# Three passes of rounded halves for the scores and values of a fused transformer's first attention

## The reference

```python
q = rms_norm((x @ wq).reshape(B, L, 16, 128), q_norm_w); k = rms_norm((x @ wk).reshape(B, L, 4, 128), k_norm_w)
v = (x @ wv).reshape(B, L, 4, 128)                        # x is the layer-normed x
k_ctx, v_ctx = rms_norm(h_ctx_kv @ wk_ctx), h_ctx_kv @ wv_ctx      # 64 context rows
q, k = rope(q), rope(k)
k_full, v_full = [k_ctx; k], [v_ctx; v]                   # 64 + 512 keys, each KV head for 4 query heads
scores = einsum('blhd,bmhd->bhlm', q, k_full) / sqrt(128) + causal mask over the 512
out = einsum('bhlm,bmhd->blhd', softmax(scores), v_full)
x = x + tanh(g_xattn[0]) * (out.reshape(B, L, 2048) @ wo)
```

## Time and profile before

| | us |
|---|---|
| median of three runs | 1883.88 |
| the profiled execution | 1885.15 |
| its span | 1883.4 |
| PE busy | 1771.8 (94%) |
| DVE busy | 1093.9 (58%) |
| ACT busy | 1041.9 (55%) |
| POOL busy | 961.5 (51%) |

### The profile page before, as it was taken

How to read it: one execution, slowest core, us unless ns; L and a number is a source line. 1 busy time by engine, 2 the same in 40 slices (tenths; PEclk the granted TensorE clock), 3 DMA queues, 4 the chain that set the end, 5 groups by cost and what they waited for, 6 DMA issues and landing times. The chain is left out here.

```text
span 1883.4 us, 27617 instructions
## 1 busy us (share of the span) xinstructions
PE 1771.8 (94%) x9732; PEld 1313.5 (70%) x9732; DVE 1093.9 (58%) x2271; ACT 1041.9 (55%) x2318; POOL 961.5 (51%) x864
## 2 busy tenths in 40 slices
PE   7899999999999999999998999989999778879998
PEld 4677777777777777777775888879899656644443
DVE  5554544456445664456655658633433668868886
ACT  3666666655555555555554322136656367857875
POOL 5644565444654445554441100038888356657774
PEclk9999999999999999999999999999999989999999
DMA  7111111211011111011121200157889660000000
GB/s 248 58 48 46 51 36 46 69 33 52 36 40 37 51 53 52 20 34 52 53 68 44 109 23 23 45 183 227 231 224 278 173 162 1 1 6 18 23 23 23
DMA packets 113607, 141.30 MB, mean 75 GB/s; under 512 B 38000, under 2 KB 68720, under 8 KB 113280
## 3 DMA queue, kind: packets, MB, share of 16 engines
q1 hardware_dynamic: 106304, 122.76, 20.7%
q0 software_dynamic: 7168, 16.78, 4.2%
HBM read 104.91 MB, written 29.36 MB: 71 GB/s over the span
## 5 line engine op out<-in xcount | busy, mean ns | idle before, releaser
L767 POOL TENSOR_TENSOR a_xcl<-xT,a_xch 128x512 fp32r<-128x512 f32 x64 | 82.9, 1295 | 282.5 <-ACT a_xch L565 282.5
L876 PE MATMUL a_S<-a_kT,a_qT 128*128 128x288 f32 (+3 forms) x640 | 207.8, 423 | 7.0 <-ACT a_qT L598 5.4
L683 DVE TENSOR_REDUCE a_nmax<-a_S 128x1 f32<-128x192 f32 (+3 forms) x256 | 138.2, 550 | 55.6 <-PE a_S L877 55.2
L934 PE MATMUL a_A<-a_pT,a_vf 128*128 128x512 f32 x320 | 167.0, 604 | 0.9 <-ACT a_pT L586 0.8
L571 ACT ACTIVATE a_pr_odd<-a_S,a_nmax 128x320 f32<-128x320 f32 (+1 forms) x128 | 80.8, 632 | 147.3 <-DVE a_nmax L683 146.0
L876 PEld LDWEIGHTS a_S<-a_kT,a_qT 128*128 128x128 f32 x640 | 115.6, 189 | 52.8 <-issue 23.6
L120 PE MATMUL a_A<-a_wlo,a_xch 128*128 128x512 f32 x256 | 147.3, 575 | 2.7 <-DVE a_qT L679 2.6
L571 ACT ACTIVATE a_pr_even<-a_S,a_nmax 128x192 f32<-128x192 f32 (+1 forms) x128 | 67.2, 527 | 121.2 <-DVE a_nmax L683 120.8
L1592 POOL TENSOR_TENSOR e_wlo<-expert_raw,e_whi 128x1408 fp32r<-128x1408 f32 x31 | 100.4, 3238 | 50.4 <-ACT e_whi L1764 48.3
L2508 PE MATMUL f_HH<-w12T,f_f_xqT 128*128 128x512 bf16 x512 | 120.0, 382 | 4.5 <-DVE a_reco L2322 2.4
L120 PE MATMUL a_A<-a_wlo,a_oth 128*128 128x512 f32 x256 | 112.1, 438 | 7.8 <-DVE a_otl L723 7.8
(11 more groups left out here) (409 smaller groups left out, 5227.6 us busy)
## 6 DMA issues: line engine op xcount, KB each, us to landing
a_pw<-in_L_ffn_w_dram SPq DMA_DIRECT2D x96, 256.0 KB, 2.9
expert_raw<-in_L_ffn_w_gate_dram SPq DMA_DIRECT2D x16, 704.0 KB, 7.6
expert_raw<-in_L_ffn_w_up_dram SPq DMA_DIRECT2D x16, 704.0 KB, 9.7
expert_raw<-in_L_ffn_w_down_dram SPq DMA_DIRECT2D x16, 512.0 KB, 10.3
tern<-a_tern SPq DMA_DIRECT2D x48, 128.0 KB, 1.9
x_res<-in_x_dram SPq DMA_DIRECT2D x4, 1024.0 KB, 9.3
a_raw<-in_L_xattn_wq_dram SPq DMA_DIRECT2D x4, 1024.0 KB, 6.6
a_raw<-in_L_xattn_wo_dram SPq DMA_DIRECT2D x4, 1024.0 KB, 5.4
```

The costliest lines, as they stand in the source:

```text
L683: ve.tensor_reduce(nmax[:, s % 2, i:i + 1], pair(s, i), AX.X, ALU.max, negate=True).then_inc(s_max, 1)
L767: pool.tensor_tensor(xcl[:, t % 2], xT[:, :, tok(t)], xch[:, t % 2].bitcast(F32), ALU.subtract).then_inc(xlo_ready, 1)
L876: pe.matmul(bank[:, lo:hi], qT[:, hq], kT[:, par(t), lo:hi], start=True, stop=hi < nk)
L934: pe.matmul(bank, vf[:, par(t), i], pT[:, i % 2], start=i == 0, stop=False)
```

## The change

Scores and values now go through `mm3`. For that each of the four operands is split: ACT's copies out of PSUM now write the rounded half (`qT_hi`, `kT_hi`, `pT_hi`), and DVE then subtracts it from the PSUM bank (new steps `t`, `k`, `G0..`) into `qT_lo`, `kT_lo`, `pT_lo`. The values go to a raw ring of three blocks (`v_raw`), are rounded by ACT into a ring of eight (`v_hi`, new step `V`) and subtracted by DVE (new step `V`). The context's keys are loaded into `kc_in` and split likewise (new step `l`, once in four slots). PE waits for the `_lo` halves where it waited for the copies, a turned block's PSUM bank is held until its `_lo` half is there, and the remainders lie in what the next stage uses as `xh` and `xl`. Weights and tables of the front lie in columns of `xT` that are written later. PE's order is the same; ACT's and DVE's have the new steps, and `j1` moves behind `t`:

```diff
-                 0: "x e0 j0 e1 g0 j1 v e2 r g1 n g2 j2 e3 g3 k t g4 o f",
+                 0: "x e0 j0 e1 g0 j1 v e2 r V g1 n g2 j2 e3 g3 k t g4 o f",
...
-    DVE_SLOT = "M0 M1 N0 L D X v M2 N1 N2 j0 j1 M3 N3 B E A"
+    DVE_SLOT = "M0 M1 N0 L D G0 X l v M2 N1 G1 N2 V j0 G2 M3 G3 N3 k t j1 G4 B E A"
...
+        v_hi = s_.sb("v_hi", [P, VRING, HD], F32R)
+        v_raw = s_.sb("v_raw", [P, 3, HD])
...
-        wvc = (pT[:, 0], pT[:, 1], vf[:, 1, 0:KVH].rearrange("p j d -> p (j d)"), kT[:, 1, 0:D])
+        wvc = [xT[:, k, 3 * L:3 * L + D] for k in range(KD)]
...
-                            act.activation(pT[:, i % 2], bank, ACT.Copy).then_inc(pT_ready, 1)
+                            act.activation(pT_hi[:, i % 2], bank, ACT.Copy).then_inc(pT_ready, 1)
...
+                    if name == "V" and live(s, 2 - i):                                        # ACT
...
+                            act.activation(v_hi[:, j % VRING], v_raw[:, j % 3], ACT.Copy).then_inc(v_hi_ready, 1)
...
+                    if name == "G" and live(s, -1) and i <= (s - 1) % BT + 1:                 # DVE
+                        t = s - 1
+                        until(ve, pT_ready, turn(i), t, m)
...
+                            ve.tensor_tensor(pT_lo[:, i % 2], bank, pT_hi[:, i % 2].bitcast(F32), ALU.subtract).then_inc(pT_lo_ready, 1)
+                    if name == "V" and live(s, 2 - i):
...
+                            ve.tensor_tensor(v_lo[:, j % VRING], v_raw[:, j % 3], v_hi[:, j % VRING].bitcast(F32),
+                                             ALU.subtract).then_inc(v_lo_ready, 1)
...
+                    if name == "t" and live(s, 1) and i == 0:
+                        t = s + 1
+                        until(ve, qT_ready, tile, t, m)
+                        ve.tensor_tensor(qT_lo, TR[:, TR_USE["T", t, 0][0]], qT_hi.bitcast(F32), ALU.subtract).then_inc(qT_lo_ready, 1)
...
-                        sem, count = {"P": (pT_ready, turn(before[2])), "T": (qT_ready, tile), "K": (kT_ready, tile),
+                        sem, count = {"P": (pT_lo_ready, turn(before[2])), "T": (qT_lo_ready, tile), "K": (kT_lo_ready, tile),
...
-                            pe.matmul(bank[:, lo:hi], qT[:, hq], kT[:, par(t), lo:hi], start=True, stop=hi < nk)
+                            mm3(pe, bank[:, lo:hi], qT_hi[:, hq], qT_lo[:, hq], kT_hi[:, par(t), lo:hi], kT_lo[:, par(t), lo:hi], True, hi < nk)
...
-                        until(pe, pT_ready, turn(i), t, m)
+                        until(pe, pT_lo_ready, turn(i), t, m)
...
-                            pe.matmul(bank, vf[:, par(t), i], pT[:, i % 2], start=i == 0, stop=False)
+                            mm3(pe, bank, v_hi[:, j], v_lo[:, j], pT_hi[:, i % 2], pT_lo[:, i % 2], i == 0, False)
```

More of the change, by code:

```diff
@@ L314, in attention0_stage @@
         wkc = odd[:, 0:KD * D].rearrange("p (k n) -> p k n", k=KD)
-        wvc = (pT[:, 0], pT[:, 1], vf[:, 1, 0:KVH].rearrange("p j d -> p (j d)"), kT[:, 1, 0:D])
[L316 to L319, removed]
+        wvc = [xT[:, k, 3 * L:3 * L + D] for k in range(KD)]
+        kc = xT[:, 0:2, 2 * L:2 * L + D].rearrange("p t (h d) -> p t h d", h=KVH)
+        causal_in = xT[:, 2, 2 * L:2 * L + P]
+        of_xh, of_xl = (home[:].rearrange("p k n -> p (k n)") for home in (xh, xl))
+        pT_lo = of_xh[:, 0:2 * GH * P].rearrange("p (u n) -> p u n", u=2)
+        v_lo = of_xh[:, 2 * GH * P:2 * GH * P + VRING * HD].rearrange("p (j d) -> p j d", j=VRING)
+        kT_lo = of_xl[:, 0:2 * KEYS].rearrange("p (u n) -> p u n", u=2)
+        qT_lo, late_lo = of_xl[:, 2 * KEYS:2 * KEYS + GH * P], of_xl[:, 2 * KEYS + GH * P:2 * KEYS + GH * P + GH * T]
         kcT = odd[:, 0:2 * D].rearrange("p (t h n) -> p t h n", t=2, h=KVH)
@@ L371, in last_block, with block_at, upper_half, by_head @@
             return i == t % BT + 1
+        def block_at(t, i):
+            return BLOCKS * (t // BT) + i
+        def upper_half(ap):
+            return ap.rearrange("p (h q) -> p h q", h=GH)[:, :, T:P]
+        def by_head(ap):
+            return ap.rearrange("p (h q) -> p h q", h=GH)
         with nc.Block() as block:
@@ L454, in _ @@
                         t = batch_next(s)
-                        if t >= 2 * BT:
-                            sp.wait_ge(o_full, tile(t - BT - 1))
+                        sp.wait_ge(ckT_lo_ready, t // BT)
+                        sp.wait_ge(v_lo_ready, block_at(t, 0) - 2)
                         load_keys(t // BT)
@@ L540, in do @@
                         act.activation(vc[:, i], A[:, A_USE["G", i, 0][0]], ACT.Copy).then_inc(cv_copied, 1)
+                    if name == "l" and live(s, 1):
+                        t = s + 1
+                        act.wait_ge(ck_loaded, 16 * batch(t))
+                        act.activation(kT_hi[:, par(t), 0:T], kc_in[:], ACT.Copy).then_inc(ckT_ready, 1)
                     if name == "y":
@@ L604, in do @@
                         act.activation(sq[:, GH], bank[:, 0:HD], ACT.Square)
-                        act.activation(vf[T:P, par(t), t % BT], bank[0:T, HD:2 * HD], ACT.Copy)
-                        act.activation(vf[0:T, par(t), t % BT + 1], bank[T:P, HD:2 * HD], ACT.Copy).then_inc(kv_act, 1)
+                        j = block_at(t, t % BT)
+                        if j > 1:
+                            act.wait_ge(v_lo_ready, j - 1)
+                        act.activation(v_raw[T:P, j % 3], bank[0:T, HD:2 * HD], ACT.Copy)
+                        act.activation(v_raw[0:T, (j + 1) % 3], bank[T:P, HD:2 * HD], ACT.Copy).then_inc(kv_act, 1)
+                    if name == "V" and live(s, 2 - i):
+                        t = s + 2 - i
+                        until(act, kv_act, tile, t, m)
+                        if t % BT == 0:
+                            act.wait_ge(cv_loaded, 16 * batch(t))
+                        for block_of in (t % BT, BT) if t % BT == BT - 1 else (t % BT,):
+                            j = block_at(t, block_of)
+                            if j >= VRING:
+                                act.wait_ge(o_full, tile(BT * ((j - VRING) // BLOCKS) + BT - 1))
+                            act.activation(v_hi[:, j % VRING], v_raw[:, j % 3], ACT.Copy).then_inc(v_hi_ready, 1)
                     if name == "f" and live(s, 2):
```

73 lines of the change are left out of this document (46 added, 27 removed), and 10 rows, old and new, of the table ACT_ORDER.

## The result

The changed kernel takes 1999.64 us (median of four runs, 1998.35 to 2003.79), the kernel before 1883.08 in the same series: ratio 1.0625, 95% interval 1.0613 to 1.0638. The profiled span grew from 1883.4 to 1997.2 us. Forecast were 1980 us and a range of 1905 to 2015.

What follows compares the result with a forecast made beforehand. PE was taken to bound the kernel, with a chain of scores, maximum, exponential and copy almost as long. 1885.15 + 55 (added steps, net) + 41 (j) = 1981, as median 1980 us; range 1905 to 2015.

Steps and rivals of the forecast that it cites:

- PE's saving: Scores and values on PE: three rounded passes instead of plain products, 59 us less work at most.
- 1 us or more: Sign of being right: PE's waits for pT_lo's subtraction before values and turned queries, this long each in nearly all slots.
- The walk through slot 30: Step-by-step timing from P0 in a kind 2 slot: V1 at 6.25 after waiting 0.75, T waits 0.8, S0 at 10.75.
- some 87%: Sign of being right: PE's busy share in the attention, down from 98.7% to this.
- The plain term: Added steps in line, all slots without the j extra: 3.45 us more per four slots, +55 us in all.
- The `j` term: Ternary pieces j0, j1 on DVE in 24 slots, delaying S0, V4 or W0: +41 us.
- I take nothing off: In the j sum of +41 us: no deduction for what may be paid before already, where j0 stands ahead of M3.
- `l`, in a gap of DVE: Context keys' split, 0.2 us in one slot of four, in a DVE gap: left at nothing.
- All hidden: Rival: the subtractions hide in DVE's idle time, all 59 us are gained, 1825 us; chance 0.06.
- Only the first wait: Rival: only a slot's first wait is real, DVE and ACT catch up behind V1, 1885 us; chance 0.08.
- Passes of 192 columns cost as much as plain products: Rival, scores of kind 0: each rounded pass takes 0.32 us, 22 us more, 2002 us; chance 0.12.
- The clock falls: Rival: the granted clock falls in PE's new waits, leading well over 2015 us; chance 0.02.

Runs made afterwards that it cites:

- the run with both parts mended: Changed kernel with PE's, ACT's and DVE's orders rewritten, P4 before T in kind 0, context keys split before the queries at the front: 1856.81 us, ratio 0.9865.
- the scores with tuned orders: Only the scores in three passes, values plain, with the rewritten orders and the remainders of key and query ahead of the output's: 1844.41 us, 0.9795 of the kernel before.

## Why the prediction was right, and where its terms were off

**The direction and the mechanism were right.** PE's saving is real (50.7 us measured, 59 at most forecast), and the waits at `V1` and `T` are there, named by the remainders' subtractions, in 46 and 44 places, 0.83 and 0.85 us long on average ("1 us or more" was too much). The walk through slot 30 gave `V1` at 6.25 behind `P0`, measured 6.18; the wait there was forecast at 0.75, measured 0.51. PE busy "some 87%" came out at 104.08 of 120. That it is where the steps stand, and not how much DVE does, the run with both parts mended shows: 143 us with no instruction less (the orders of PE and ACT by themselves gave the kernel before 16).

**The plain term was right.** From `P0` to `S0` slots 28, 21, 22 and 31, of kinds 0 to 3 and without `j` on DVE, grew by 1.30, 0.73, 1.02 and 1.03 us; the walk had 1.35, 0.55, 0.9 and 1.1. In slot 22 `T` starts 8.66 behind `P0` after a wait of 0.70, and the next `S0` 10.86 behind (walked: 8.55, 0.8, 10.75). From score to score slots 12, 21, 22 and 23 grew by 1.48, 0.66, 0.88 and 0.70: 3.72 for four slots where 3.45 were forecast, 59 us in the 63. Slots 33 and 49 stand out, with 1.8 (their next `S0` waits 1.65 us for the query's remainder), and those behind them with 0.3; why is open.

**One price in it was wrong, in six slots.** The values' subtraction was priced like any of 128 columns. Beside a POOL instruction it takes longer (last section), and so it does in slots 13, 14, 29, 30, 45 and 46, which together grew by 4 us more than slots 21 and 22 did:

- In slot 30 it took 0.99 us, in slot 22 0.27. All behind it came 0.7 later: `T` at 9.25, forecast 8.55.
- In slot 29, of kind 1, `T` starts 5.77 behind `P0`, as the walk had it (5.75). But the values' two subtractions take 1.58 us, in slot 21 0.47; `M3` stands behind them, the fourth exponential and the query's copy behind that, and the query's remainder is 0.92 us late for `S0`, which does not wait in slot 21.

On PE the `S0` at the end of slot 21, `T` of slot 22, and `T` and the next `S0` of slot 29; on DVE the values' subtractions of slots 21 and 22, and slot 29:

```profile
414.91 0.47 PE L120 MATMUL a_S<-xl,a_qT_hi 128*128 128x448 f32 x1
...
427.94 0.63 PE L1003 MATMUL a_TR<-ident_f,a_qa 128*128 128x128 f32 x4 [0.70 <-DVE xl L665]
...
546.19 0.63 PE L1003 MATMUL a_TR<-ident_f,a_qa 128*128 128x128 f32 x4 [0.78 <-DVE xl L665]
550.15 0.47 PE L120 MATMUL a_S<-xl,a_qT_hi 128*128 128x448 f32 x1 [0.92 <-DVE xl L775]
```

```profile
411.65 0.47 DVE L674 TENSOR_TENSOR xh<-a_v_raw,a_v_hi 128x128 fp32r<-128x128 f32 x2
...
425.40 0.27 DVE L674 TENSOR_TENSOR xh<-a_v_raw,a_v_hi 128x128 fp32r<-128x128 f32 x1
...
546.04 1.58 DVE L674 TENSOR_TENSOR xh<-a_v_raw,a_v_hi 128x128 fp32r<-128x128 f32 x2
547.55 0.48 DVE L732 TENSOR_REDUCE a_nmax<-a_S 128x1 f32<-128x320 f32 x1
...
549.41 0.68 DVE L775 TENSOR_TENSOR xl<-a_TR,a_qT_hi 128x512 fp32r<-128x512 f32 x1
```

**The `j` term was too large.** The 24 slots cost 50.4 us; at the growth of slots 12, 21, 22 and 23 they would have cost 23, so 27 are left, and 4 more in slots 28, 44 and 60, where `B` comes late behind the `j1` of the slot before. That is 31 where 41 were forecast. "I take nothing off" was the wrong choice: the slots with `j` were already longer before (slot 30, of kind 2, 14.35 us; the mean of kind 2 with `j` 15.13), by some 10 us in the 24. So the price of the pieces was about right in the sum, though not kind by kind: with `j`, kind 1 grew no more than without. Moving the pieces gave back 35, so it also took away a part of what was paid before.

**Not seen**: `X` behind `G0` (16.9 us of waits for the normalised rows, 9 us by the run that moved it), and the context's keys' remainder, "`l`, in a gap of DVE", for which the first `S0` waits 4.1 us. Together: 59 + 31, 4 for the stretched subtractions, 13 more in the 16 slots with sums (ten of which have `X`), 6 at the ends, 1 elsewhere: 114, the growth of the span. The forecast's 96 was nearly right in its largest term, 10 us too high in `j` and without the 24 us that it had not seen; that these partly cancel was luck.

**The rivals.** *All hidden* (1825): with the subtractions gone altogether these orders gave 1859, so it could not have come true by hiding them; with better orders 1817. *Only the first wait* (1885): `T` waits 37.2 us in 44 slots. *Passes of 192 columns cost as much as plain products*: one of 192 columns is followed by the next after 0.09 to 0.12 us, not 0.32:

```profile
521.09 0.25 PE L120 MATMUL a_S<-xl,a_qT_hi 128*128 128x192 f32 x1
521.18 0.28 PE L121 MATMUL a_S<-a_kT_hi,xl 128*128 128x192 f32 x1
521.29 0.27 PE L122 MATMUL a_S<-a_kT_hi,a_qT_hi 128*128 128x192 f32 x1
521.41 0.23 PE L940 MATMUL a_S<-a_causal,a_ident_b 128*128 128x128 bf16 x1
```

Three take 0.32, as long as the plain product did; the prediction had priced them at 0.26, 0.088 each. By the Trainium skill (TensorE: Matmul & The Clock Gate, section LDWEIGHTS) loading 128 columns of weights takes about columns/1.2 ns, an estimated 107 ns. The second and third pass, 0.11 to 0.12 us, agree with it as a lower bound of their distance; the rows of the weight loads themselves (PEld) are 0.19 us long. *The clock falls*: it does, in seven of the 108 stretches of 10 us between 40 and 1120 us, in six falls. One stands behind a wait of 4.1 us and two behind waits of 2.1, though the prediction had no new wait over 2 us, one behind 1.5 and two behind pairs of 0.9 to 1.0. It loses at most 12 us of full speed (the shares missing from 1.00 times 10 us), so the price "well over 2015" was too high.

## What to carry to other kernels

On in-order engines a step costs what stands behind it, so a step that waits for another engine belongs behind everything that doesn't need it: price each added step by the next instruction that somebody waits for, through to the end of the slot, and not only up to the first wait. Test such a walk on several slots: slot 30 alone would have blamed the walk for what a neighbour on POOL does in six slots. Before giving up a saving of the bounding engine for lost overlap, write the orders of all engines anew, and give the kernel before the same orders: here that turned +117 us into -26, and showed that 16 us of it were the orders' own. And look at each part by itself: the scores with tuned orders beat both parts by 12 us, so there the values' remainders cost more than their passes save.

## What the runs showed of the hardware

**DVE held by POOL.** The subtraction of two operands in SBUF (L674) takes 0.27 us, but 0.99 in slot 30, where POOL runs a subtraction of its own from 560.19 to 561.47; DVE's ends 0.15 us later:

```profile
560.19 1.28 POOL L830 TENSOR_TENSOR a_xcl<-xT,a_xch 128x512 fp32r<-128x512 f32 x1
```

In slot 29 the two of 1.58 us end 0.14 us after a POOL instruction (L846, 546.70 to 547.48). Of the 79 rows of L674 and of L765, the context's keys (17 rows hold two subtractions), 24 are stretched; all of them begin while a POOL instruction runs and end 0.07 to 0.15 us after it, or, in four, after the one that POOL began next. Of the 55 others, one begins beside a POOL instruction, a short one of 5 columns. It is 16 us of DVE's time in all, some of it on the path. Subtractions out of PSUM show none of it: L668 takes 0.68 to 0.69 us in all 160, 58 of which begin beside a POOL instruction. The Trainium skill (SBUF — State Buffer, section SBUF: two separate sides) has the rule: a DVE instruction with two inputs in SBUF and a GpSimd instruction that reads SBUF take a shared port in turns, each for its whole length. The trace agrees; no run takes POOL's instructions away, so what it costs the kernel was not measured.

**The clock after short waits.** At 480.42 and 482.30 PE came out of waits of 0.97 and 0.92 us, and then passes of 512 columns stand 0.43 us apart instead of 0.23, the 1.2 GHz level, up to 486.3:

```profile
480.42 0.47 PE L120 MATMUL a_S<-xl,a_qT_hi 128*128 128x448 f32 x1 [0.97 <-DVE xl L775]
...
482.30 0.47 PE L120 MATMUL a_A<-a_wlo,a_oth 128*128 128x512 f32 x1 [0.92 <-DVE a_otl L786]
...
482.94 0.63 PE L122 MATMUL a_A<-a_whi,a_oth 128*128 128x512 f32 x1
483.36 0.63 PE L120 MATMUL a_A<-a_wlo,a_oth 128*128 128x512 f32 x1
```

The windows view has it as a granted clock of 0.83 in that stretch; in the kernel before no stretch of 10 us from 40 to 1010 us, in which its 64 slots lie, is below 1.00.

```profile
480.00:490.00 10.00, 8.65 (x41) 6.78 (x41) 6.70 (x12) 3.61 (x10) 6.28 (x6) 0.83 0.18 61
```
